# A fused group-norm and windowed-attention kernel: exponentials split by pairs of tiles, row sums moved to a bank of the row scores, the statistic put before the second maximum, the bias of V put on ScalarE

## The chip, the cores and the metric

The kernel runs on one core of a Trainium2 chip. The metric is device time in microseconds (us) of one execution, lower is better. PE is TensorE (PEld its weight loads), DVE is VectorE, ACT is ScalarE, POOL is GpSimd, SP is the engine that issues the DMAs.

## The reference

The input is x of shape (4, 128, 112, 112) in fp32. It is group-normalised (32 groups of 4 channels per image), goes through attention in shifted windows, and is added to the result. Cut to what matters:

```python
def _gn(v, G=32, eps=1e-05):           # mean and variance per image and group
    ...
xs = jnp.roll(x, (-3, -3), axis=(-2, -1))
qkv = jnp.einsum('bchw,oc->bohw', xs, w_qkv) + b_qkv[None, :, None, None]
# 16 x 16 windows of 7 x 7 = 49 tokens, 8 heads of 16 channels
scores = jnp.einsum('bxyhqd,bxyhkd->bxyhqk', q, k) * scale
attn = jax.nn.softmax(scores, axis=-1)
out = jnp.einsum('bxyhqk,bxyhkd->bxyhqd', attn, v)
...
x = x + _L0_conv_ref(_gn(x), w_qkv, b_qkv)
```

## The kernel before, in words

An image is 16 bands of 7 rows, and a band is two groups of 8 windows. So there are 4 x 32 = 128 groups, and the program is a software pipeline over them: each engine runs its own list of work, `step(g)`, in an order written out by hand, and semaphores (one counter for each kind of result, waited for with `wait_ge`) tie the lists together. PE's order sets the beat. In its step g it does, in this order:

- `project_v(g)` (L725), V of group g into the V bank,
- `sum_keys(g-2)` (L783), the sums of the exponentials over the keys, 64 fp32 matmuls (rows of the trace),
- `weigh(g-2)` (L797), exponentials times V,
- `project_q(g+1)` (L716),
- `row_scores(g, 0)` (L740), the scores of heads 0 to 3 with a query in each row, needed only for the row maximum; it waits for the masked queries (`q_masked`) and for K split in two halves (`k_split`),
- `turn_max(g-1)` (L752), `spread_inverse(g-2)` (L808),
- `column_scores(g-1)` (L765, L772), the scores again with a key in each row, the negated maximum added,
- `row_scores(g, 1)` (L740), and `project_k(g+1)` (L709).

DVE's step g: `mask_q(g)` (L564, two instructions), the statistic of the next image (`take_stats`, L487, one chunk of 448 elements; a step has one chunk, two, or none), `invert(g-2)` (L576) and `low_inverse(g-2)` (L581), `join(g-2)` (L588), `maximum(g, 0)` (L571), `low_q(g+1)` (L556), `scale_rows(g-2)` (L597), `maximum(g, 1)` (L571). ACT's step: `evac_k`, `normalise(g+2)`, `high_inverse`, `evac_even`, `evac_v`, `evac_q(g+1)`, `evac_neg(g-1)` (L368), and the two exponentials of g-1 (L373). POOL's step: `add_bias(g-3)` (L291, the bias of V added to the output), `split_max(g-1)` (L282, L285), `split_k(g)` (L273, L275: k_hi, then k_lo = k - k_hi, whose end is `k_split`), `add_image(g-3)` (L300, the residual), `split_x(g+2)` (L263, L265).

The statistics of image b+1 are gathered while image b is worked on: 28 chunks of `take_stats`, then the chain of small instructions that turns them into scale and shift. `change_image` cuts that chain over six steps, in pieces that stand at two places of the step, before `invert` (`ahead`) and before `join` (`between`). Steps 22 to 29, 54 to 61 and 86 to 93 are the eight before each new image is needed; the last image, from step 94 on, has no statistics left to take.

PSUM has 8 banks. Row scores use banks 0 and 1, Q and K bank 4, V, the turned maximum and the spread inverse bank 5. Heads 0 and 1 of the column scores are in banks 6 and 7, heads 2 and 3 in banks 2 and 3, so the first exponential (`exp(g, 0)`) takes heads 0 and 1 of all four pairs of windows, the second heads 2 and 3. The sums over the keys lie in spare columns of bank 3; `weigh` writes banks 6 and 7. SP stores each band and loads one of a later image in its place.

Of the kernel before, what the change touches and what calls it, by code (L numbers as in the profile page):

```python
# [35 lines left out]
def window_attention(nc, x, w_qkv, b_qkv, out):  # L36
# [7 lines left out]
    with ctx:  # L44
# [181 lines left out]
        def _(pool):  # L226
# [61 lines left out]
            def add_bias(g, half):  # L288
                pool.wait_ge(mixed_done, g + 2)
                pool.sem_inc(waited, 1)  # L290
                nc.gpsimd.tensor_scalar(mixed[:, half, :, :], mixed[:, half, :, :], bias[:, 2:3], None, ALU.add).then_inc(bias_added, 1)  # L291

# [24 lines left out]
            for g in range(-2, 4):  # L317
                step(g, g // 2, g & 1)
            with pool.Fori(2, GROUPS // 2 - 1) as n:
# [4 lines left out]
            for g in range(GROUPS - 2, GROUPS + 3):  # L324
                step(g, g // 2, g & 1)

        @block.scalar
        def _(act):
# [23 lines left out]

            def evac_k(g):
# [38 lines left out]
            def step(g, n, par, b=0):  # L392
# [12 lines left out]
                if live(g - 1):  # L405
                    evac_neg(g - 1)
                if live(g - 1):
# [16 lines left out]
            for g in range(GROUPS - 2, GROUPS + 2):  # L424
# [3 lines left out]
        def _(dve):  # L428
# [87 lines left out]
            def group_mean():  # L516
# [4 lines left out]
                link(nc.vector.tensor_tensor(work_b[:, :], work_a[:, :], work_a[:, :], ALU.mult))  # L521

            def group_variance():

                link(nc.vector.tensor_tensor(work_a[:, :], work_b[:, :], var_row[:, :], ALU.add))
# [3 lines left out]
            def guess_root():  # L529

# [3 lines left out]
            def refine_root(steps):  # L534

                for _ in range(steps):
                    link(nc.vector.tensor_tensor(rs_t[:, :], rs[:, :], rs[:, :], ALU.mult))
                    link(nc.vector.scalar_tensor_tensor(rs_t[:, :], rs_t[:, :], -0.5, g_var[:, :], ALU.mult, ALU.mult))
                    link(nc.vector.scalar_tensor_tensor(rs[:, :], rs_t[:, :], 1.5, rs[:, :], ALU.add, ALU.mult))

            def scatter_groups():
# [4 lines left out]
            def offer(b):  # L546

                wait(dve, xn_ready, (b - 1) * 2 * BANDS)
# [52 lines left out]
            def step(g, n, par, chunks=(), image_at=None, ahead=None, between=None):  # L601
# [11 lines left out]
                if between:  # L613
                    between()
# [6 lines left out]
                if live(g - 2):  # L621
                    scale_rows(g - 2, par)
                if live(g):
# [7 lines left out]
            def change_image(b):  # L631

                g = (b * BANDS - 4) * 2
                for ahead, between in ((None, lambda: gather_channels(b)),
                                       (turn_channels, group_mean),
                                       (group_variance, guess_root),
                                       (lambda: refine_root(1), lambda: refine_root(1)),
                                       (lambda: refine_root(NEWTON - 2), scatter_groups),
                                       (None, lambda: offer(b))):
                    step(g, g // 2, g & 1, ahead=ahead, between=between)  # L640
                    g += 1
# [9 lines left out]
            gather_channels(0)  # L651
            turn_channels()
            group_mean()
            group_variance()
            guess_root()
            refine_root(NEWTON)
            scatter_groups()
            offer(0)
# [5 lines left out]
            step(2, 1, 0)  # L664
            step(3, 1, 1)
            with dve.Fori(2, BANDS - 4) as n:
# [196 lines left out]
```

## Time and profile before

| | |
|---|---|
| median of 3 runs | 941.21 us (940.23 to 943.64) |
| the profiled execution | 941.08 us, its span 938.9 us |
| PE busy (matmul) | 865.0 us, 92% of the span |
| DVE busy | 766.3 us, 82% |
| POOL busy | 739.3 us, 79% |
| ACT busy | 665.1 us, 71% |
| DMA | 51.87 MB, mean 55 GB/s |

The span is the time from the first to the last instruction on the chip; the execution's own time is 2.2 us more. The shares of busy time are averages over the fill of the pipeline (some 72 us), 124 steps and a short drain. A busy PE here is the union of matmuls whose ends are modelled, so 92% doesn't say that PE is the only limit: two steps of the same work are best compared by their length. Line numbers are those of the kernel before.

### The profile page before, as it was taken

To read this page: it belongs to the slowest core of one execution; us is meant where nothing else is said; L and a number is where in the kernel's file an instruction comes from. 1 tells how busy PE (TensorE), PEld (TensorE's weight loads), DVE (VectorE), ACT (ScalarE), POOL (GpSimd) and SP (SyncE) were. 2 spreads that over 40 slices of the span, in tenths; PEclk is the share of its full clock that TensorE was granted. 3 is DMA by queue.
4 is the path that set the end of the run, shared out by engine and by line. 5 is a ranking of instruction groups with operands and counts; after the bars stand their busy time and mean duration, and the time that the engine had idled before them with its cause. 6 is when DMAs were issued, how large, how long until landed. Compare 5 with 4: busy or idle time off the path is not lost. (4 is left out here: it accounts for less than half of the span.)

```text
span 938.9 us, 104445 instructions
## 1 busy us (share of the span) xinstructions
PE 865.0 (92%) x46473; PEld 708.7 (75%) x46473; DVE 766.3 (82%) x1399; ACT 665.1 (71%) x1297; POOL 739.3 (79%) x1191
## 2 busy tenths in 40 slices
PE   0479999998999999999999999999899999999994
PEld 0358888887788888887788888887678888888883
DVE  8657888889889888888888888888987777777873
ACT  2347777776677777777677777777677777777772
POOL 1347888887788888888788888888788888888883
PEclk9999999999999999999999999999999999999998
DMA  9401122112112211221211000000000000000001
GB/s 380 177 5 58 46 68 68 60 42 69 48 55 68 69 43 60 68 68 34 69 54 50 35 34 34 17 34 34 17 34 35 19 32 34 34 22 29 34 34 36
DMA packets 29912, 51.87 MB, mean 55 GB/s; under 512 B 3649, under 2 KB 28865, under 8 KB 29761
## 3 DMA queue, kind: packets, MB, share of 16 engines
q1 hardware_dynamic: 29888, 51.59, 15.8%
q8 instruction: 11, 0.18, 0.1%
q14 instruction: 13, 0.10, 0.0%
HBM read 25.89 MB, written 25.69 MB: 55 GB/s over the span
## 5 line engine op out<-in xcount | busy, mean ns | idle before, releaser
L373 ACT ACTIVATE probs_t<-psum,exp_scale 128x800 f32<-128x800 f32 x256 | 223.2, 923 | 139.6 <-PE psum L772 139.6
L571 DVE TENSOR_REDUCE neg_max<-psum 100x16 f32<-100x784 f32 x256 | 249.2, 974 | 39.1 <-PE psum L740 31.1
L291 POOL TENSOR_SCALAR mixed<-mixed,bias 128x392 f32<-128x392 f32 x128 | 161.7, 1263 | 123.2 <-DVE mixed L597 123.2
L740 PEld LDWEIGHTS psum<-k_hi,q_masks 32*128 32x128 f16 x8192 | 175.3, 91 | 46.3 <-issue 42.8
L740 PE MATMUL psum<-k_hi,q_masks 32*128 32x49 f16 x8192 | 197.8, 179 | 3.0 <-DVE neg_max L571 2.3
L740 PE MATMUL psum<-k_lo,q_masks 32*128 32x49 f16 x4096 | 182.6, 179 | 0.0
L740 PEld LDWEIGHTS psum<-k_lo,q_masks 32*128 32x128 f16 x4096 | 161.0, 91 | 0.0
L300 POOL TENSOR_TENSOR stage<-mixed,image 128x343 f32 (+7 forms) x256 | 144.2, 583 | 0.4 <-POOL mixed L291 0.4
L765 PE MATMUL psum<-q_masks,k_hi 32*64 32x100 f16 x8192 | 128.7, 219 | 16.1 <-DVE summed L588 13.3
L349 ACT ACTIVATE xn<-image,shift_c,rstd_c 128x21 f32 (+6 forms) x256 | 132.4, 573 | 8.0 <-DVE shift_c L551 6.1
L797 PE MATMUL psum<-probs_t,v_rows 64*32 64x100 f32 x8192 | 131.4, 252 | 2.4 <-issue 2.4
L783 PE MATMUL psum<-probs_t,sum_rows 128*32 128x49 f32 x8192 | 117.7, 209 | 9.6 <-ACT probs_t L373 2.7
L783 PEld LDWEIGHTS psum<-probs_t,sum_rows 128*32 128x32 f32 x8192 | 103.8, 110 | 28.5 <-issue 25.2
L275 POOL TENSOR_TENSOR k_lo<-k,k_hi 128x392 f16<-128x392 f32 x128 | 116.5, 910 | 10.7
L265 POOL TENSOR_TENSOR xn_lo<-xn,xn_hi 128x392 f16<-128x392 f32 x128 | 116.2, 908 | 10.7
L564 DVE TENSOR_SCALAR q_masks<-q_halves,even_odd 128x800 f16<-128x800 f16 x256 | 120.6, 511 | 2.3 <-DMA image<-in_x_dram 2.3
L765 PEld LDWEIGHTS psum<-q_masks,k_hi 32*64 32x64 f16 x8192 | 103.5, 102 | 22.5 <-issue 17.8
L765 PE MATMUL psum<-q_masks,k_lo 32*64 32x100 f16 x4096 | 111.7, 218 | 0.0
L797 PEld LDWEIGHTS psum<-probs_t,v_rows 64*32 64x32 f32 x8192 | 102.5, 106 | 11.4 <-issue 2.8
L588 DVE SCALAR_TENSOR_TENSOR summed<-psum,v_scale,even_out 128x392 f32<-128x392 f32 x128 | 80.1, 625 | 38.1 <-ACT even_out L390 37.4
L725 PE MATMUL psum<-w_lo,xn_hi 128*128 128x128 f16 x512 | 94.9, 222 | 0.0
L725 PE MATMUL psum<-w_hi,xn_lo 128*128 128x128 f16 x512 | 94.8, 222 | 0.0
(112 smaller groups left out, 1828.2 us busy)
## 6 DMA issues: line engine op xcount, KB each, us to landing
out_dram<-stage SPq DMA_DIRECT2D x64, 224.0 KB, 2.1
out_dram<-stage SPq DMA_DIRECT2D x64, 168.0 KB, 1.9
image<-in_x_dram SPq DMA_DIRECT2D x32, 224.0 KB, 2.6
image<-in_x_dram SPq DMA_DIRECT2D x1, 6104.0 KB, 28.2
image<-in_x_dram SPq DMA_DIRECT2D x34, 168.0 KB, 2.5
image<-in_x_dram SPq DMA_DIRECT2D x6, 896.0 KB, 9.2
image<-in_x_dram SPq DMA_DIRECT2D x1, 728.0 KB, 14.3
w_nat<-in_L_conv_w_qkv_dram SPq DMA_DIRECT2D x1, 192.0 KB, 2.4
```

What stands on the lines that cost most here:

```text
L275: nc.gpsimd.tensor_tensor(k_lo[:, par, :, 0:TOK], k, k_hi[:, par, :, 0:TOK], ALU.subtract).then_inc(k_split, 1)
L291: nc.gpsimd.tensor_scalar(mixed[:, half, :, :], mixed[:, half, :, :], bias[:, 2:3], None, ALU.add).then_inc(bias_added, 1)
L300: last = nc.gpsimd.tensor_tensor(pixel_view(stage[:, bass.ds(st, BAND)], piece), token_view(mixed[:, half, :, :], piece), pixel_view(image ...
L349: last = nc.scalar.activation(token_view(xn, piece), pixel_view(image[:, bass.ds(at, BAND)], piece), ACT.Identity, bias=shift_c[:, b % 2:b ...
L373: nc.scalar.activation(probs_t[:, 2 * u:2 * u + 2, :, :].rearrange("p h a q -> p h (a q)"), psum[:, COL_BANKS[u], 0:PAIRS * ROWS2], ACT.Ex ...
L564: last = nc.vector.tensor_scalar(both[:, :, e, :], q_halves[:, :, :, :].rearrange("p l w q -> p (l w) q"), even_odd[:, e:e + 1], None, ALU ...
L571: nc.vector.tensor_reduce(neg_max[:, par, 2 * j:2 * j + 2, :], psum[0:ROWS2, ROW_BANKS, 0:GT] .rearrange("p h (w k) -> p h w k", k=TOK), A ...
L725: last = nc.tensor.matmul(psum[:, V_BANK, a * C:(a + 1) * C], xs[:, par, 2 * a:2 * a + 2, :].rearrange("p w k -> p (w k)"), wv[:, 2, :], s ...
L740: last = nc.tensor.matmul(psum[:, ROW_BANKS.start + h - 2 * j, w * TOK:(w + 1) * TOK], q_masks[rows, par, low + w * ROWS2:low + w * ROWS2 ...
L765: nc.tensor.matmul(psum[side, COL_BANKS[h // 2].start + h % 2, a * ROWS2:(a + 1) * ROWS2], k[rows, par, w, :], q_masks[rows, par, low + w ...
L783: last = nc.tensor.matmul(psum[c * PC:(c + 1) * PC, SUM_BANK, SPARE_SUM], sum_rows[:, a, e, :, :, :].rearrange("p t w s -> p (t w s)"), pr ...
L797: last = nc.tensor.matmul(psum[c * PC:(c + 1) * PC, OUT_BANKS.start + s, a * C:a * C + ROWS2], v_rows[side, par, a, c * PC:(c + 1) * PC], ...
```

## The change

Five things are edited together.

1. The banks are dealt anew: column scores in banks 4 to 7 (one for each of the four pairs of heads), V, turned maximum and inverse in bank 3, Q and K in bank 2. An exponential now covers all heads of two pairs of windows: `exp(g, 0)` pairs 0 and 1, `exp(g, 1)` pairs 2 and 3; each still reads 800 elements per partition. `sum_keys` waits for the first before its first matmul, and for the second in its middle.
2. The sums over the keys lie in the spare columns of bank 0, beside row scores. So `sum_keys(g-2)` waits for the second maximum of g-1 (`max_done[1]`), `row_scores(g, 0)` waits for `inv_done` of g-2, and `column_scores` no longer does.
3. `take_stats` and every piece of the chain (`ahead`) stand right before the second maximum; the place `between` is gone. `change_image` has eight steps in place of six, and starts two steps earlier. A step's chunks are dealt a little differently: steps 2 and 3 take one, and the four steps before each of the last two changes of image take two each (eight such steps), where before four steps in all took two.
4. `add_bias` goes from POOL to ACT, behind `evac_neg` and ahead of the exponentials.
5. `add_image` on POOL works on g-4 in place of g-3, and the pipeline's end gets a step more.

The diff, cut to its core:

```diff
-        ROW_BANKS, COL_BANKS, OUT_BANKS = slice(0, 2), (slice(6, 8), slice(2, 4)), slice(6, 8)
-        NEG_BANK, SUM_BANK, QK_BANK, V_BANK, INV_BANK = 5, 3, 4, 5, 5
+        ROW_BANKS, COL_BANKS, OUT_BANKS = slice(0, 2), slice(4, 8), slice(6, 8)
+        NEG_BANK, SUM_BANK, QK_BANK, V_BANK, INV_BANK = 3, 0, 2, 3, 3
-        SPARE_SUM = slice(PAIRS * ROWS2, PAIRS * ROWS2 + TOK)
+        SPARE_SUM = slice(GT, GT + TOK)
+        HALF = PAIRS // 2
...
             def step(g, n, par):
-                if live(g - 3):
-                    add_bias(g - 3, 1 - par)
...
-                if live(g - 3):
-                    add_image(g - 3, n - 2 + par, 1 - par)
+                if live(g - 4):
+                    add_image(g - 4, n - 2, par)
...
+            def add_bias(g, half):
+                act.wait_ge(mixed_done, g + 2)
+                nc.scalar.activation(mixed[:, half, :, :], mixed[:, half, :, :], ACT.Identity, bias=bias[:, 2:3]).then_inc(bias_added, 1)
...
-                nc.scalar.activation(probs_t[:, 2 * u:2 * u + 2, :, :].rearrange("p h a q -> p h (a q)"),
-                                     psum[:, COL_BANKS[u], 0:PAIRS * ROWS2], ACT.Exp, scale=exp_scale[:, 0:1]).then_inc(exp_done[u], 1)
+                nc.scalar.activation(probs_t[:, :, u * HALF:(u + 1) * HALF, :].rearrange("p h a q -> p h (a q)"),
+                                     psum[:, COL_BANKS, u * HALF * ROWS2:(u + 1) * HALF * ROWS2], ACT.Exp,
+                                     scale=exp_scale[:, 0:1]).then_inc(exp_done[u], 1)
...
                     evac_neg(g - 1)
+                if live(g - 3):
+                    add_bias(g - 3, 1 - par)
                 if live(g - 1):
                     exp(g - 1, 0)
...
+            def norm_steps(b):
+                return [lambda: gather_channels(b), turn_channels, group_mean, group_variance] + NEWTON * [refine_root] + [lambda: offer(b)]
...
                 if live(g):
                     mask_q(g, par)
-                if ahead:
-                    ahead()
-                for chunk in chunks:
-                    take_stats(image_at + chunk * STAT, chunk)
                 if live(g - 2):
                     invert(g - 2)
                     low_inverse(g - 2)
-                if between:
-                    between()
...
                 if live(g - 2):
                     scale_rows(g - 2, par)
+                if ahead:
+                    ahead()
+                for chunk in chunks:
+                    take_stats(image_at + chunk * STAT, chunk)
                 if live(g):
                     maximum(g, par, 1)
...
+                first = (b * BANDS - 5) * 2
+                for g, piece in enumerate(norm_steps(b), first):
+                    step(g, g // 2, g & 1, ahead=piece)
...
             def row_scores(g, par, j):
...
                     pe.wait_ge(k_split, g + 1)
+                    wait(pe, inv_done, g - 1)
...
             def column_scores(g, par):
                 wait(pe, exp_done[1], g)
-                wait(pe, inv_done, g)
...
             def sum_keys(g):
-                pe.wait_ge(exp_done[0], g + 1)
-                pe.wait_ge(exp_done[1], g + 1)
+                pe.wait_ge(max_done[1], min(g + 2, GROUPS) if isinstance(g, int) else g + 2)
                 for a in range(PAIRS):
+                    if a % HALF == 0:
+                        pe.wait_ge(exp_done[a // HALF], g + 1)
```

The program of DVE in the second step of a pass through its loop over the first image. Before, from the masks of one step to its second maximum:

```order
L564 TENSOR_SCALAR q_masks<-q_halves,even_odd 128x16x50 [waits col_mm,q_low]
L564 TENSOR_SCALAR q_masks<-q_halves,even_odd 128x16x50
L487 ISA x2
L487 BN_STATS stats<-image 128x6
L576 RECIPROCAL inv<-psum 128x49 [waits sum_mm]
L581 SCALAR_TENSOR_TENSOR inv_rows<-inv_hi,low_rows,inv 128x49 [waits inv_mm,inv_high]
L588 SCALAR_TENSOR_TENSOR summed<-psum,v_scale,even_out 128x392 [waits mixed_done,even_done]
L571 TENSOR_REDUCE neg_max<-psum 100x16 [waits neg_split,row_mm_0]
L555 REGISTER_ALU
L556 SCALAR_TENSOR_TENSOR q_halves<-psum,q_bias,q_halves 128x8x49 [waits q_high]
L597 TENSOR_TENSOR mixed<-psum,summed 128x2x4x49 [waits join_done,add_done,neg_ready,inv_mm]
L571 TENSOR_REDUCE neg_max<-psum 100x16 [waits neg_split,row_mm_1]
```

And with the change, in the same step (line numbers of the changed kernel):

```order
L561 TENSOR_SCALAR q_masks<-q_halves,even_odd 128x16x50 [waits col_mm,q_low]
L561 TENSOR_SCALAR q_masks<-q_halves,even_odd 128x16x50
L573 RECIPROCAL inv<-psum 128x49 [waits sum_mm]
L578 SCALAR_TENSOR_TENSOR inv_rows<-inv_hi,low_rows,inv 128x49 [waits inv_mm,inv_high]
L585 SCALAR_TENSOR_TENSOR summed<-psum,v_scale,even_out 128x392 [waits mixed_done,even_done]
L568 TENSOR_REDUCE neg_max<-psum 100x16 [waits neg_split,row_mm_0]
L552 REGISTER_ALU
L553 SCALAR_TENSOR_TENSOR q_halves<-psum,q_bias,q_halves 128x8x49 [waits q_high]
L594 TENSOR_TENSOR mixed<-psum,summed 128x2x4x49 [waits join_done,add_done,neg_ready,inv_mm]
L488 ISA x2
L488 BN_STATS stats<-image 128x6
L568 TENSOR_REDUCE neg_max<-psum 100x16 [waits neg_split,row_mm_1]
```

The statistic and the two instructions that set its addresses moved from behind the masks to between `scale_rows` and the second maximum.

The program of POOL at the start of a step of its loop. Before:

```order
L291 TENSOR_SCALAR mixed<-mixed,bias 128x392 [waits mixed_done]
L282 TENSOR_SCALAR neg_halves<-neg_max 100x4x8 [waits neg_mm,max_done_0,max_done_1]
L285 TENSOR_TENSOR neg_halves<-neg_max,neg_halves 100x4x8 [waits neg_high]
L269 REGISTER_ALU
L273 TENSOR_SCALAR k_hi<-k 128x8x49 [waits k_evac,col_mm]
L275 TENSOR_TENSOR k_lo<-k,k_hi 128x8x49 [waits k_high]
```

And with the change:

```order
L283 TENSOR_SCALAR neg_halves<-neg_max 100x4x8 [waits neg_mm,max_done_0,max_done_1]
L286 TENSOR_TENSOR neg_halves<-neg_max,neg_halves 100x4x8 [waits neg_high]
L270 REGISTER_ALU
L274 TENSOR_SCALAR k_hi<-k 128x8x49 [waits k_evac,col_mm]
L276 TENSOR_TENSOR k_lo<-k,k_hi 128x8x49 [waits k_high]
```

The bias is gone from the head of POOL's step; the split of the maximum, which waits for the second maximum, is the step's first instruction.

## Rows read from the trace of the kernel before

**Rows 1.** Windows of whole steps, L588 alone (one per step): us, DVE busy (x), clock, DMA

```profile
99.42:199.78 100.36, 9.39 (x15) 1.00 0.18 59
691.66:912.48 220.82, 20.67 (x33) 1.00 0.08 30
193.09:251.52 58.43, 5.00 (x8) 1.00 0.18 55
412.76:471.88 59.12, 4.99 (x8) 0.97 0.17 54
633.09:691.66 58.57, 5.00 (x8) 1.00 0.08 28
291.69:305.65 13.96, 1.23 (x2) 1.00 0.18 58
```

**Rows 2.** Timeline of one step with a statistic, PE's loads: start us, us, instruction

```profile
406.76 0.10 PEld L725 LDWEIGHTS psum<-w_lo,xn_hi 128*128 128x128 f16 x1
407.06 0.80 PEld L783 LDWEIGHTS psum<-probs_t,sum_rows 128*32 128x32 f32 x64 [0.20 <-issue]
...
409.49 0.10 PEld L740 LDWEIGHTS psum<-k_hi,q_masks 32*128 32x128 f16 x2 [0.33 <-issue]
```

**Rows 3.** Timeline of the same step, ACT

```profile
405.20 1.74 ACT L373 ACTIVATE probs_t<-psum,exp_scale 128x800 f32<-128x800 f32 x2 [0.95 <-PE psum L772]
```

**Rows 4.** Timeline of the fill, PE's loads from V to the sums

```profile
51.33 0.10 PEld L725 LDWEIGHTS psum<-w_lo,xn_hi 128*128 128x128 f16 x1
...
51.53 0.58 PEld L783 LDWEIGHTS psum<-probs_t,sum_rows 128*32 128x32 f32 x46
```

**Rows 5.** Timeline of the step of rows 2, DVE

```profile
405.04 0.56 DVE L597 TENSOR_TENSOR mixed<-psum,summed 128x392 f32<-128x392 f32 x1
405.79 0.97 DVE L571 TENSOR_REDUCE neg_max<-psum 100x16 f32<-100x784 f32 x1 [0.19 <-PE psum L740]
406.68 0.94 DVE L564 TENSOR_SCALAR q_masks<-q_halves,even_odd 128x800 f16<-128x800 f16 x2
407.55 0.61 DVE L487 BATCH_NORM_STATS2 stats<-image  x1
408.08 0.45 DVE L576 RECIPROCAL inv<-psum 128x49 f32<-128x49 f32 x1
```

**Rows 6.** Timeline of the same step, POOL

```profile
405.81 1.26 POOL L291 TENSOR_SCALAR mixed<-mixed,bias 128x392 f32<-128x392 f32 x1 [0.56 <-DVE mixed L597]
...
407.04 0.32 POOL L282 TENSOR_SCALAR neg_halves<-neg_max 100x32 bf16<-100x32 f32 x1
...
408.31 0.91 POOL L275 TENSOR_TENSOR k_lo<-k,k_hi 128x392 f16<-128x392 f32 x1
```

**Rows 7.** Timeline of the fill, a step of POOL without the bias, and the masks

```profile
60.75 0.76 DVE L564 TENSOR_SCALAR q_masks<-q_halves,even_odd 128x800 f16<-128x800 f16 x2
61.01 0.57 POOL L282 TENSOR_SCALAR neg_halves<-neg_max 100x32 bf16<-100x32 f32 x1 [1.59 <-DVE neg_max L571]
...
62.48 0.91 POOL L275 TENSOR_TENSOR k_lo<-k,k_hi 128x392 f16<-128x392 f32 x1
```

**Rows 8.** Timeline of the fill, k_lo and the row scores that wait for it

```profile
44.80 0.91 POOL L275 TENSOR_TENSOR k_lo<-k,k_hi 128x392 f16<-128x392 f32 x1
...
45.77 0.13 PEld L740 LDWEIGHTS psum<-k_hi,q_masks 32*128 32x128 f16 x2 [1.00 <-issue]
```

**Rows 9.** Timeline of the start, DVE: the chain's first instruction, and the one after its last

```profile
22.64 0.92 DVE L507 BATCH_NORM_AGGREGATE agg<-stats 128x2 f32<-128x168 f32 x1
...
28.44 0.21 DVE L478 TENSOR_SCALAR q_bias<-bias,fit 128x1 f32<-128x1 f32 x1
```

**Rows 10.** Groups by line and shape: busy us, mean ns, idle before

```profile
L390 ACT ACTIVATE even_out<-psum,v_scale 128x392 f32<-128x392 f32 x128 | 75.1, 587 | 20.8 <-PE psum L797 14.6
```

**Rows 11.** Timeline of the drain

```profile
931.53 0.57 DVE L597 TENSOR_TENSOR mixed<-psum,summed 128x392 f32<-128x392 f32 x1 [0.20 <-DVE summed L588]
932.31 1.26 POOL L291 TENSOR_SCALAR mixed<-mixed,bias 128x392 f32<-128x392 f32 x1 [5.51 <-DVE mixed L597]
933.76 1.26 POOL L300 TENSOR_TENSOR stage<-mixed,image 128x343 f32<-128x343 f32 x3 [0.18 <-POOL mixed L291]
```

More of the change, by code:

```diff
@@ L286, in split_max @@
                                         ALU.subtract).then_inc(neg_split, 1)
[L288 to L291, printed above, removed]
             def add_image(g, t, half):
@@ L311, in step @@
                     split_k(g, par)
-                if live(g - 3):
-                    add_image(g - 3, n - 2 + par, 1 - par)
+                if live(g - 4):
+                    add_image(g - 4, n - 2, par)
                 if live(g + 2):
                     split_x(g + 2, par)
-            for g in range(-2, 4):
+            for g in range(-2, 6):
                 step(g, g // 2, g & 1)
-            with pool.Fori(2, GROUPS // 2 - 1) as n:
+            with pool.Fori(3, GROUPS // 2 - 1) as n:
                 step(2 * n, n, 0)
@@ L323, in _ @@
             pool.sem_inc(x_split, 1)
-            for g in range(GROUPS - 2, GROUPS + 3):
+            for g in range(GROUPS - 2, GROUPS + 4):
                 step(g, g // 2, g & 1)
@@ L423, in _ @@
                     step(2 * n + 1, n, 1, b)
-            for g in range(GROUPS - 2, GROUPS + 2):
+            for g in range(GROUPS - 2, GROUPS + 3):
                 step(g, g // 2, g & 1)
@@ L599, in scale_rows, with step @@
                                         summed[:, :, :].rearrange("p (s a) q -> p s a q", s=2), ALU.mult).then_inc(mixed_done, 1)
-            def step(g, n, par, chunks=(), image_at=None, ahead=None, between=None):
+            def step(g, n, par, chunks=(), image_at=None, ahead=None):
                 if live(g):
                     mask_q(g, par)
-                if ahead:
-                    ahead()
-                for chunk in chunks:
-                    take_stats(image_at + chunk * STAT, chunk)
                 if live(g - 2):
@@ L650, in _ @@
                     take_stats(chunk * STAT, chunk)
[L651 to L658, printed above, removed]
+            for piece in norm_steps(0):
+                piece()
             work_out_scales()
@@ L663, in _ @@
             step(1, 0, 1, range(5, 8), BANDS * BAND)
-            step(2, 1, 0)
-            step(3, 1, 1)
-            with dve.Fori(2, BANDS - 4) as n:
-                two_steps(n, 2 * n + 4, BANDS * BAND)
+            step(2, 1, 0, (8,), BANDS * BAND)
+            step(3, 1, 1, (9,), BANDS * BAND)
+            with dve.Fori(2, BANDS - 5) as n:
+                two_steps(n, 2 * n + 6, BANDS * BAND)
             for b in (1, 2):
@@ L671, in _ @@
                 first = b * BANDS - 1
-                for n in range(3):
+                for n in range(4):
                     dve.wait_ge(loaded[b + 1], 32 * -(-(2 * n + 2) * STAT // BAND))
@@ L675, in _ @@
                 dve.wait_ge(loaded[b + 1], 32 * BANDS)
-                for g in (2 * first + 6, 2 * first + 7):
-                    chunk = 6 + 2 * (g & 1)
-                    step(g, g // 2, g & 1, (chunk, chunk + 1), at)
-                with dve.Fori(4, CHUNKS // 2 - 1) as n:
-                    two_steps(n + first, 2 * n + 2, at)
+                with dve.Fori(4, CHUNKS // 2 - 4) as n:
+                    two_steps(n + first, 2 * n, at)
+                for n in (CHUNKS // 2 - 4, CHUNKS // 2 - 3):
+                    for par in range(2):
+                        chunk = CHUNKS - 8 + 4 * (n - CHUNKS // 2 + 4) + 2 * par
+                        step(2 * (first + n) + par, first + n, par, (chunk, chunk + 1), at)
             change_image(B - 1)
@@ L764, in column_scores @@
                                 rows = slice(h * PC, (h + 1) * PC)
-                                nc.tensor.matmul(psum[side, COL_BANKS[h // 2].start + h % 2, a * ROWS2:(a + 1) * ROWS2], k[rows, par, w, :],
+                                nc.tensor.matmul(psum[side, COL_BANKS.start + h, a * ROWS2:(a + 1) * ROWS2], k[rows, par, w, :],
                                                  q_masks[rows, par, low + w * ROWS2:low + (w + 1) * ROWS2],
@@ L771, in column_scores @@
                         rows = slice(h * PC, (h + 1) * PC)
-                        last = nc.tensor.matmul(psum[:, COL_BANKS[h // 2].start + h % 2, a * ROWS2:(a + 1) * ROWS2],
+                        last = nc.tensor.matmul(psum[:, COL_BANKS.start + h, a * ROWS2:(a + 1) * ROWS2],
                                                 pick_window[rows, 2 * a:2 * a + 2, :].rearrange("p w k -> p (w k)"),
```

26 lines of the change are left out of this document (7 added, 19 removed).

## The prediction

> **What bounds the kernel now.** The page gives PE 92% and DVE 82% busy, which settles nothing, so I first cut the span into whole steps. One L588 runs per step, so its count in a window gives the length of a step [rows 1]: 15 steps with one statistic take 100.36 us, 6.69 each, and the last 33 steps, which have none, take 220.82 us, 6.69 each. A statistic on DVE costs nothing where it stands now. The eight steps before a change of image take 58.43, 59.12 and 58.57 us, together 16 us more than 24 such steps, and two steps with two statistics take 13.96, 0.58 more than two plain ones.
>
> What sets the 6.69 is read from the timeline of one step. PE goes through its phases with short gaps, and the question is which gaps are waits. From V to the sums, load to load, it takes 0.30 (406.76 to 407.06) [rows 2], and the second exponential ends at 405.20 + 1.74 = 406.94, 0.12 before [rows 3]. In the fill, with the exponentials long done, the same pair of loads is 0.20 apart [rows 4]. So 0.10 of each step is a wait for the second exponential, and the rest of the step is PE's own pace.
>
> Two other chains come close. DVE: the second maximum ends at 405.79 + 0.97 = 406.76, 0.30 before the sums [rows 5]. POOL: k_lo ends at 408.31 + 0.91 = 409.22, and the row scores start at 409.49 [rows 2, 6]. In the fill PE took up the row scores 0.06 after k_lo (45.71 to 45.77), so in a plain step k_lo has 0.27 - 0.07 = 0.20 to spare [rows 8].
>
> **The exponentials by pairs.** The first now frees the sums 0.8 earlier, the second is needed only after half of their 0.80. Each still has 800 elements, so I leave 1.74 for both. The wait goes, 0.10 per step, where nothing else is late; no step can gain more, since 0.20 is what the fill shows without a wait.
>
> **The sums in a bank of the row scores.** They now wait for the second maximum as well. It is done at 406.76, and the sums could load at 406.96: nothing in a plain step. The inversion that the next row scores wait for starts at 408.08 and lasts 0.45, a good 0.9 before them: nothing.
>
> **The bias on ACT.** An ACT pass over 392 elements takes 0.59 [rows 10]. It stands where ACT now waits 0.95 for the column scores [rows 3]; the `mixed` that it reads is a step old. The price lies between nothing and, if it took even 0.9, still nothing: I take nothing. `add_image`, a step later, is ready long before `scale_rows` needs its buffer back.
>
> **The bias off POOL.** This frees 1.26 per step, but what counts is the end of k_lo. Before, the bias runs over the first mask; the split of the maximum starts at 407.04 and k_lo ends 2.54 after the masks start (406.68) [rows 5, 6]. The fill has the same steps without a bias [rows 7]: the masks start at 60.75 and end at 61.51, L282 asks at 61.01 and needs 0.57 in place of 0.32, ending just after both masks, and k_lo ends at 63.39, 2.64 after they started. So without the bias POOL is kept out by both masks, and k_lo comes 0.10 **later**, not earlier. I take the fill's value; the bound on the other side is rival 1. In a plain step k_lo then allows the row scores 0.20 - 0.10 = 0.10 earlier than now, exactly what the exponentials give. A plain step: 6.59, and 34 of them save 34 x 0.10 = 3.4.
>
> The Trainium skill (SBUF — State Buffer, § Who interferes with whom) says that DVE in a two-port mode and GpSimd share a port pair, and that "whoever issues first gets the shared pair for the whole instruction". By that rule L282, asking while the first mask holds the pair and before the second has started, would get in between the two, and the whole would end near rival 1's time. The row at 61.01 doesn't agree on this point: it ends behind the second mask.
>
> **The statistic before the second maximum.** Every step that has one pays here. `scale_rows` starts at 405.04 and ends at 405.60; an instruction that waits for nothing starts 0.08 before its predecessor's end, so the statistic starts at 405.52. Start to start it takes 408.08 - 407.55 = 0.53, call it 0.54, and the maximum starts at 406.06 in place of 405.79: 0.27 late [rows 5]. Behind it are queued the masks, and for it wait the sums on PE and the split of the maximum on POOL. The sums: the maximum ends at 407.03, with some 0.06 on top 407.09, 0.03 later than now. k_lo: 0.27 + 0.10 late, less the 0.20 to spare, 0.17. The second is the larger, and PE loses it once (the 0.03 lies inside). A step with one statistic: 6.69 + 0.17 = 6.86. There are 58 past the fill (4 to 21, 30 to 49, 62 to 81): 58 x 0.17 = +9.9.
>
> In general a step whose piece takes p before the maximum costs p - 0.37 more than 6.69. Two statistics, p = 1.07: +0.70, 8 such steps, +5.6. The pairs of before are given back: 2 x 0.58, -1.2.
>
> **The chain at the changes of image.** Its eight pieces now stand there, in eight steps. Their bound from below is the start of the program, where DVE runs the same chain with nothing beside it: 22.64 to 28.44, 5.80 in all [rows 9]. I take it, since POOL has done its L265 by then. Eight steps: 8 x 6.69 + 5.80 - 8 x 0.37 = 56.4, three times 169.1 in place of 176.1: -7.0.
>
> **Fill and drain.** The fill's first statistics delay one maximum and free an earlier one; I take 0, with 3 either way. At the end the last `mixed` is done at 932.10 and the residual starts at 933.76, with 1.26 of bias between; with 0.59 on ACT it is 0.7 less [rows 11].
>
> **Sum.** 9.9 + 5.6 - 1.2 - 7.0 - 3.4 - 0.7 = +3.2 on the profiled execution's 941.08, so **944.3 us**. That execution is 0.1 under the median of 941.21. Within 0.5% (4.7 us) is about what a measurement can't tell from no change: 936.5 to 945.9. So the forecast is no change, on its slow side.
>
> **Rivals.**
> *1. POOL gets in between the masks.* The split of the maximum is then as fast as now, after a start of 0.14 less: k_lo about 0.2 earlier than I have it, and only the sums bind. Steps with one statistic +0.03 (1.7), with two +0.57 (4.6), changes of image 3 x (8 x 6.69 + 5.80 - 8 x 0.51) = 165.7 (-10.4), the others as above (-5.3): -9.4, **931.7**. For it: in a step with the bias L282 takes 0.32 and ends before the masks do. Against: the fill's row. Chance 0.20.
>
> *2. The statistic costs more than its own time.* In the loops two instructions that set its address precede it. If they aren't worked off under `scale_rows`, each such step pays their time before the maximum. Behind the masks they cost nothing (407.55 is 0.07 before the masks' end); the other bound is the 0.20 that DVE idles where it waits for its own last result [rows 11]. With 0.2 on 66 steps: +13, **957**. It decides early: 0.02 per step takes the time out of the 0.5%. Chance 0.12.
>
> *3. The split of the exponentials does nothing,* because the wait in the middle of the sums, or the one for the maximum at their head, holds PE as long as before. Plain steps stay at 6.69: +3.4, **947.7**. Chance 0.08.
>
> **How the numbers follow.** The forecast has 0.60, of which I give 0.40 to within 0.5%, 0.18 to slower (each 0.03 in the statistic's 0.17 is 2 us) and 0.02 to faster. Rival 1 is faster with 0.20, rival 2 slower with 0.12, rival 3 slower with 0.05 and within with 0.03. Together: faster 0.22, same 0.43, slower 0.35. The range runs from rival 1's time, rounded down, to 955, which leaves out the upper part of rival 2. The forecast's own range is 940 to 949.
>
> **What would show it.** Windows of whole steps: 6.59 in the last image, 6.86 with a statistic, 7.39 with two, 56.4 for eight steps at a change. L283 (the old L282) at about 0.57, ending behind both masks. In steps with a statistic, row scores that load 0.06 after k_lo's end, a second maximum that has no idle time before it, and no idle time of PE before the sums but for their 0.1. If L283 takes 0.3 and steps with a statistic 6.72, rival 1 holds; if the statistic starts well after `scale_rows` ends, rival 2; if the last image stays at 6.69, rival 3.

## The result, and the profile after

| | before | changed |
|---|---|---|
| median | 941.21 us (940.23 to 944.43, 5 runs) | 948.05 us (946.93 to 949.03, 5 runs) |
| the profiled execution, and its span | 941.08, 938.9 | 947.95, 946.1 |
| PE, DVE busy | 865.0, 766.3 us | 867.6, 765.6 us |
| ACT, POOL busy | 665.1, 739.3 us | 731.6, 599.0 us |

The changed kernel is slower, by little: the ratio is 1.0065, 95% interval 1.0042 to 1.0088. Over one execution the busy times tell nothing of this; POOL even lost 140 us of work. The windows of whole steps do. Here they are for the changed kernel, one L585 per step (us, DVE busy with its count, clock, DMA share, GB/s): twelve steps with one statistic, the last 33, the eight before each change of image, and four with two statistics.

```profile
101.13:183.68 82.55, 7.51 (x12) 1.00 0.19 58
701.34:920.89 219.55, 20.64 (x33) 1.00 0.08 30
197.46:253.86 56.40, 5.01 (x8) 1.00 0.18 57
420.64:477.58 56.94, 5.01 (x8) 1.00 0.17 56
644.41:701.34 56.93, 5.01 (x8) 1.00 0.08 28
391.59:420.64 29.05, 2.51 (x4) 1.00 0.17 55
```

Against [rows 1] a step with one statistic grew from 6.69 to 6.88 us, a plain step shrank from 6.69 to 6.65 (6.64 past its first), the eight steps at a change went from some 58.7 to 56.8, and a step with two statistics takes 7.26 (7.40 each, measured past the first). Each window runs from V's first load of one step to that of another. What stands before the second maximum in step g delays PE's loads of step g+1, so the first length in a window is still that of the kind of step before it.

The clock is the full 2.4 GHz in all six windows (1.00), so it has no part in the longer steps. In the kernel before, one of the three changes of image holds 3.4 us at 1.2 GHz (455.9 to 459.3; its window has 0.97 in [rows 1]) and takes 0.6 more than the other two: that much of the changed kernel's gain there isn't the change's. In the fill the clock does differ: between V's first load and that of step 4 it is 0.80 on average in the changed kernel, 0.93 in the kernel before.

The timeline of one step with a statistic (start us, us, instruction) answers to [rows 2, 5, 6]; V's first load of this step is at 329.66:

```profile
329.14 0.62 DVE L488 BATCH_NORM_STATS2 stats<-image  x1
329.67 0.96 DVE L568 TENSOR_REDUCE neg_max<-psum 100x16 f32<-100x784 f32 x1
...
330.54 0.76 DVE L561 TENSOR_SCALAR q_masks<-q_halves,even_odd 128x800 f16<-128x800 f16 x2
...
330.68 0.77 PEld L768 LDWEIGHTS psum<-probs_t,sum_rows 128*32 128x32 f32 x64 [0.20 <-DVE neg_max L568]
...
330.81 0.56 POOL L283 TENSOR_SCALAR neg_halves<-neg_max 100x32 bf16<-100x32 f32 x1 [2.06 <-DVE neg_max L568]
...
332.30 0.91 POOL L276 TENSOR_TENSOR k_lo<-k,k_hi 128x392 f16<-128x392 f32 x1
...
333.28 0.12 PEld L725 LDWEIGHTS psum<-k_hi,q_masks 32*128 32x128 f16 x2 [0.53 <-issue]
```

Read it from the top. The second maximum starts right behind the statistic, with no idle time, where before it had 0.19 of it. It ends at 330.63, and the sums on PE load 0.05 later, their wait now put down to it. The split of the maximum (L283) starts at 330.81, lasts 0.56 and ends at 331.37, 0.07 after the masks (331.30). k_lo ends at 333.21, and the row scores load 0.07 after. Their wait reads as "issue", not as POOL: only that it grew from 0.33 [rows 2] to 0.53, and always ends 0.07 after k_lo, tells that it is one.

A plain step, V's first load at 741.61, has the same pattern without the statistic. k_lo ends at 744.92, 2.66 after the masks start, and the row scores load 0.07 later:

```profile
742.26 0.76 DVE L561 TENSOR_SCALAR q_masks<-q_halves,even_odd 128x800 f16<-128x800 f16 x2
...
742.54 0.77 PEld L768 LDWEIGHTS psum<-probs_t,sum_rows 128*32 128x32 f32 x64
742.68 0.41 POOL L283 TENSOR_SCALAR neg_halves<-neg_max 100x32 bf16<-100x32 f32 x1 [1.68 <-DVE neg_max L568]
...
744.01 0.91 POOL L276 TENSOR_TENSOR k_lo<-k,k_hi 128x392 f16<-128x392 f32 x1
...
744.99 0.12 PEld L725 LDWEIGHTS psum<-k_hi,q_masks 32*128 32x128 f16 x2 [0.38 <-issue]
```

From the page's groups (busy us, mean ns of one, idle before): L283 takes 489 ns on average, where L282 took 332 in the kernel before, and the exponentials are as long as they were, 924 ns against 923.

```profile
L371 ACT ACTIVATE probs_t<-psum,exp_scale 128x800 f32<-128x800 f32 x256 | 223.5, 924 | 60.2 <-PE psum L756 60.2
L283 POOL TENSOR_SCALAR neg_halves<-neg_max 100x32 bf16<-100x32 f32 x128 | 62.6, 489 | 273.5 <-DVE neg_max L568 273.5
```

At the drain the residual starts 0.83 after the last `mixed`, in place of 1.66 [rows 11]:

```profile
939.58 0.57 DVE L594 TENSOR_TENSOR mixed<-psum,summed 128x392 f32<-128x392 f32 x1 [0.20 <-DVE summed L585]
...
940.98 1.27 POOL L296 TENSOR_TENSOR stage<-mixed,image 128x343 f32<-128x343 f32 x3 [0.26 <-ACT mixed L349]
```

### The profile page after: what moved, and what is told of

Same layout as the page of the kernel before. It is cut to its first block, busy times and chain, and to the rows that moved or that the text cites. A ratio compares the mean times of both kernels' runs of the same rounds, so it can differ in the third digit from the quotient of the medians.

```text
span 946.1 us, 104227 instructions
## 1 busy us (share of the span) xinstructions
PE 867.6 (92%) x46473; PEld 706.4 (75%) x46473; DVE 765.6 (81%) x1399; ACT 731.6 (77%) x1425; POOL 599.0 (63%) x1063
## 4 chain that ended last, share of the span: by engine, by line
PE 80%; DVE 10%; issue 5%; DMA 3%; ACT 1%; SPq 1%; POOL 0%; DVEq 0%; POOLq 0%; ACTq 0%
PE psum L725 17%; PE psum L782 13%; PE psum L768 12%; PE psum L749 10%; PE psum L700 8%; PE psum L709 7%; PE psum L693 6%; DVE neg_max L568 4%; DMA image<-in_x_dram 3%; PE psum L756 3%; PE psum L737 2%; PE psum L793 2%; DVE q_halves L553 2%; DVE mixed L594 2%; DVE stats L488 1%
## 5 line engine op out<-in xcount | busy, mean ns | idle before, releaser
L283 POOL TENSOR_SCALAR neg_halves<-neg_max 100x32 bf16<-100x32 f32 x128 | 62.6, 489 | 273.5 <-DVE neg_max L568 273.5
L725 PEld LDWEIGHTS psum<-k_hi,q_masks 32*128 32x128 f16 x8192 | 177.9, 91 | 66.6 <-issue 64.2
L578 DVE SCALAR_TENSOR_TENSOR inv_rows<-inv_hi,low_rows,inv 128x49 f16<-128x49 f16 x128 | 90.4, 706 | 49.1 <-ACT inv_hi L383 49.1
L768 PEld LDWEIGHTS psum<-probs_t,sum_rows 128*32 128x32 f32 x8192 | 99.7, 110 | 35.1 <-DVE neg_max L568 27.4
L573 DVE RECIPROCAL inv<-psum 128x49 f32<-128x49 f32 x128 | 60.2, 470 | 59.9 <-PE psum L768 59.9
L561 DVE TENSOR_SCALAR q_masks<-q_halves,even_odd 128x800 f16<-128x800 f16 x256 | 97.7, 425 | 2.6 <-DMA image<-in_x_dram 2.6
```

The costliest lines, as they stand in the source:

```text
L561: last = nc.vector.tensor_scalar(both[:, :, e, :], q_halves[:, :, :, :].rearrange("p l w q -> p (l w) q"), even_odd[:, e:e + 1], None, ALU ...
L725: last = nc.tensor.matmul(psum[:, ROW_BANKS.start + h - 2 * j, w * TOK:(w + 1) * TOK], q_masks[rows, par, low + w * ROWS2:low + w * ROWS2 ...
L768: last = nc.tensor.matmul(psum[c * PC:(c + 1) * PC, SUM_BANK, SPARE_SUM], sum_rows[:, a, e, :, :, :].rearrange("p t w s -> p (t w s)"), pr ...
```

## The experiments

The theory on trial (A) is the prediction's: the time goes through one chain, second maximum, masks, split of the maximum, k_lo, row scores; the statistic in front makes it start late, and the bias gone from POOL lets the masks' hold on POOL make it longer. The rivals are that the new banks and waits cost it, that the sums' wait for the maximum is the whole loss, and that taking work off POOL did shorten the chain. e1 to e4 ran on one chip beside 14 runs of the kernel before (median 942.25), e5 to e8 beside 12 (941.89), e9 beside 9 (940.56). The ratios below are against these. A difference from the changed kernel's 948.05 crosses sessions, whose medians of the kernel before lie within 1.7 us of each other (941.21 beside the 948.05), so it is good to a us or two; the windows of steps are firmer.

**e1, the statistic back behind the masks.** All else as in the changed kernel.

```diff
                     mask_q(g, par)
+                for chunk in chunks:
+                    take_stats(image_at + chunk * STAT, chunk)
...
                     ahead()
-                for chunk in chunks:
-                    take_stats(image_at + chunk * STAT, chunk)
```

> The changed kernel with the statistic's chunks back behind the masks; the pieces of the chain stay before the second maximum. Theory A (the changed kernel loses its time because the statistic delays the second maximum, and with it the masks, the split of the maximum on POOL, k_lo and the row scores): single-statistic steps fall from 6.88 us to the 6.64 of plain steps, two-statistic steps from 7.40 to about 6.94; 58 x 0.24 + 8 x 0.46 = 17.6 less than the changed kernel, about 930 us. Theory B (the loss comes from the new banks, the bias on ACT or the wait of the sums for the maximum): about as the changed kernel, 946 to 950.

929.21 us (927.69 to 929.44), ratio 0.9856 [0.9834, 0.9879]. Twelve steps with a statistic (first row) and the last 33:

```profile
100.54:180.20 79.66, 7.52 (x12) 1.00 0.19 60
683.74:903.24 219.50, 20.68 (x33) 1.00 0.08 30
```

Both kinds of step take 6.64. So the place of the statistic costs the changed kernel some 18.8 us, and without that one edit it beats the kernel before by 1.4%. Theory B of this run falls.

**e2, K's split ahead of the maximum's on POOL.** The statistic stays where the change put it.

```diff
             def step(g, n, par):
-                if live(g - 1):
-                    split_max(g - 1, 1 - par)
                 if live(g):
                     split_k(g, par)
+                if live(g - 1):
+                    split_max(g - 1, 1 - par)
```

> The changed kernel with POOL's split of K ahead of its split of the maximum; nothing else moves. Theory A (k_lo sets the row scores, and it is late because it is queued behind a split that waits for the late maximum and for the masks' port): k_lo no longer depends on the maximum, so only the sums' wait for the maximum is left: plain steps 6.59 to 6.60 in place of 6.64, single-statistic steps about 6.72 in place of 6.88, two statistics about 7.25, eight steps at a change about 55.2 in place of 56.8; about 932 to 933 us. L283 short, under 0.2 us. Theory B (the sums' wait for the late maximum is the loss, k_lo only follows): single-statistic steps stay at 6.85 to 6.88, time 947 to 948. Danger: the split of the maximum comes late for turn_max, then steps grow.

924.14 us (923.43 to 925.21), ratio 0.9805 [0.9783, 0.9827]. Windows as above, and the timeline of a step with a statistic (V's first load at 313.85):

```profile
98.75:178.64 79.89, 7.51 (x12) 1.00 0.19 60
681.46:898.32 216.86, 20.64 (x33) 1.00 0.08 31
```

```profile
314.74 0.75 DVE L561 TENSOR_SCALAR q_masks<-q_halves,even_odd 128x800 f16<-128x800 f16 x2
314.88 0.77 PEld L768 LDWEIGHTS psum<-probs_t,sum_rows 128*32 128x32 f32 x64 [0.20 <-DVE neg_max L568]
...
316.13 0.91 POOL L276 TENSOR_TENSOR k_lo<-k,k_hi 128x392 f16<-128x392 f32 x1
317.01 0.22 POOL L283 TENSOR_SCALAR neg_halves<-neg_max 100x32 bf16<-100x32 f32 x1
...
317.28 0.09 PEld L725 LDWEIGHTS psum<-k_hi,q_masks 32*128 32x128 f16 x2 [0.33 <-issue]
```

k_lo now ends at 317.04, 0.24 before the row scores, which are back at an idle time of 0.33. Steps with a statistic fall to 6.66, and what is left over the plain 6.56 is the sums' wait for the late maximum, 0.10. So of the 0.24 that a statistic cost, k_lo's chain carried most, and the order on POOL alone is worth 23.9 us. It came out 8 us better than expected, in good part because PE's own pace is 6.56, not 6.59, and steps with a statistic take 6.66, not 6.72. The sums' loads take 0.77 in place of 0.80 [rows 2]. They do so here too, where they wait for the maximum; in e5, where they wait for the second exponential again, they take 0.80.

**e3, both edits.**

> Both edits: statistic behind the masks, K's split ahead of the maximum's. Theory A: plain and single-statistic steps all at PE's own pace, 6.59 to 6.60, two-statistic steps under 6.95, changes of image about 55.2 per eight steps: about 922 to 924 us, faster than both kernels. Theory B: no better than the better of the two edits alone by more than 1 us.

916.39 us (915.21 to 917.44), ratio 0.9721 [0.9702, 0.9739].

```profile
99.50:178.22 78.72, 7.51 (x12) 1.00 0.19 61
673.74:890.60 216.86, 20.64 (x33) 1.00 0.08 31
```

Every step of one statistic or none takes 6.56, PE's own pace. 7.8 us better than e2 alone.

**e4, the bias back on POOL**, at the head of its step as in the kernel before, all else as in the changed kernel.

```diff
+                if live(g - 3):
+                    add_bias(g - 3, 1 - par)
                 if live(g - 1):
                     split_max(g - 1, 1 - par)
```

ACT no longer adds it.

> The changed kernel with the bias of V back on POOL, at the head of its step. Theory A (without the bias POOL's split of the maximum meets both masks and waits them out; with it the split comes in between them): plain steps fall to about 6.60 with L282's work at about 0.3 us in place of 0.49, steps with a statistic stay near 6.88, since there the split is asked for later and meets the masks all the same; about 945 to 947 us. Theory B (the bias was in POOL's way, and taking it off shortened the chain to k_lo): plain steps grow to 6.7 or more, over 950 us.

939.56 us (936.87 to 940.7), ratio 0.9961 [0.9942, 0.9979]. The timeline of a step with a statistic (V's first load at 319.81):

```profile
319.58 1.26 POOL L292 TENSOR_SCALAR mixed<-mixed,bias 128x392 f32<-128x392 f32 x1 [0.47 <-DVE mixed L595]
...
320.70 0.76 DVE L562 TENSOR_SCALAR q_masks<-q_halves,even_odd 128x800 f16<-128x800 f16 x2
...
320.96 0.23 POOL L283 TENSOR_SCALAR neg_halves<-neg_max 100x32 bf16<-100x32 f32 x1
...
322.15 0.91 POOL L276 TENSOR_TENSOR k_lo<-k,k_hi 128x392 f16<-128x392 f32 x1
...
323.24 0.09 PEld L726 LDWEIGHTS psum<-k_hi,q_masks 32*128 32x128 f16 x2 [0.33 <-issue]
```

With 1.26 us more to do per step, POOL finishes k_lo earlier: 2.36 after the masks start in place of 2.67, because L283 takes 0.23 and is done at 321.19, before the masks' end at 321.46. Moving the bias off POOL cost some 8.5 us in all. That is less than the steps alone would make it, for eight steps at a change are longer here, 57.9 to 58.6 against 56.4 to 56.9. I had the gain for plain steps only (6.56 measured, expected 6.60), and expected steps with a statistic to stay at 6.88; they fell to 6.66. In them L283 starts 0.07 before the second mask, just as in the changed kernel, and yet it gets in, in all 58 of them. Where two statistics or a piece of the chain stand in the step it doesn't, at the same distance. Here is one such step; the bias ended 0.64 before the split's start, not 0.11:

```profile
394.47 0.76 DVE L562 TENSOR_SCALAR q_masks<-q_halves,even_odd 128x800 f16<-128x800 f16 x2
394.73 0.57 POOL L283 TENSOR_SCALAR neg_halves<-neg_max 100x32 bf16<-100x32 f32 x1 [0.64 <-DVE neg_max L569]
```

e8 and e9 go after that.

**e5, both exponentials waited for ahead of the sums.**

```diff
-                for a in range(PAIRS):
-                    if a % HALF == 0:
-                        pe.wait_ge(exp_done[a // HALF], g + 1)
+                pe.wait_ge(exp_done[0], g + 1)
+                pe.wait_ge(exp_done[1], g + 1)
+                for a in range(PAIRS):
```

> The changed kernel with both exponentials waited for at the head of the sums. Theory A (the split of the exponentials is worth its 0.10 us where nothing else is late, and where a statistic makes the maximum late, nothing): the sums load at 1.02 after V's first load in plain steps in place of 0.93, row scores would start at 3.45 in place of 3.38, so plain steps 6.69 in place of 6.64 and steps with a statistic unchanged at 6.88: 34 x 0.05 = +1.7, about 950 us. Theory B (the wait in the middle of the sums costs as much as it gives): unchanged, 948 us, plain steps 6.64.

950.83 us (948.17 to 952.0), ratio 1.0096 [1.0076, 1.0116], 2.8 over the changed kernel's median; by the time alone the two can't be told apart. The last 33 steps, and the sums of one of them:

```profile
701.99:923.21 221.22, 20.67 (x33) 1.00 0.08 30
```

```profile
743.51 0.80 PEld L768 LDWEIGHTS psum<-probs_t,sum_rows 128*32 128x32 f32 x64 [0.20 <-issue]
```

The 33 plain steps make 1.7 of it. They go back to the 6.69 of before, those with a statistic stay (6.87). So the split does what it says, for 0.05 us a plain step here; the other 0.08, down to 6.56, it gives only where k_lo isn't late.

**e6, one part alone on the kernel before:** bias on ACT and residual on g-4, nothing else.

> The kernel before with nothing but the bias of V on ACT and the residual on g-4. Theory A (without the bias ahead of it POOL's split of the maximum waits both masks out, and k_lo comes about 0.10 us later, which here lies inside the 0.20 it has to spare): plain steps 6.69, L282's work about 0.5 us in place of 0.32, time 940 to 942 us, less some 0.7 to 1.2 at the drain; the bias as such is worth nothing to the steps. Theory B (freeing POOL of 1.26 us per step makes k_lo and the steps faster): steps under 6.65, under 937 us.

945.52 us (943.68 to 947.6), ratio 1.004 [1.0027, 1.0053]. The last 33 steps, the group of the split, and DVE at step 36:

```profile
699.23:920.11 220.88, 20.67 (x33) 1.00 0.08 30
```

```profile
L282 POOL TENSOR_SCALAR neg_halves<-neg_max 100x32 bf16<-100x32 f32 x128 | 62.0, 484 | 273.0 <-DVE neg_max L570 273.0
```

```profile
295.46 1.68 DVE L563 TENSOR_SCALAR q_masks<-q_halves,even_odd 128x800 f16<-128x800 f16 x2 [1.99 <-DMA image<-in_x_dram]
```

Steps stay at 6.69, with L282 at 484 ns: k_lo's delay lies inside what it had to spare, as theory A has it, and the steps gain nothing from POOL's free time. The time is 4 us more all the same, from a cost I hadn't counted: with the residual a step later, bands are stored and loaded later (the load that ends this wait is issued at 292.81, in step 36, where the kernel before issues it at 284.96, at the end of step 34), and DVE waits at steps 36 and 68 for the last band of the next image. Those two steps take 10.81 and 11.13. Behind each wait the clock is 1.2 GHz for a while, which is part of the cost:

```profile
300.70:304.00 3.30, 3.30 (x141) 2.58 (x133) 2.22 (x5) 2.31 (x4) 0.00 (x0) 0.50 0.00 0
522.50:529.20 6.70, 6.56 (x236) 5.62 (x240) 4.78 (x9) 4.78 (x9) 2.00 (x4) 0.50 0.00 0
```

(us, then busy time of PE, PE's loads, DVE, ACT and POOL, and the clock.) The changed kernel asks for the band two steps later, at steps 38 and 70, and has no such wait: its new dealing of chunks spares it this.

**e7, the chain's pieces behind the masks too**, on top of e3.

```diff
                     mask_q(g, par)
+                if ahead:
+                    ahead()
...
-                if ahead:
-                    ahead()
```

> The fastest so far (statistic behind the masks, K's split ahead of the maximum's) with the chain's pieces behind the masks too, one per step in eight steps. Theory A (behind the masks a step has some 0.8 us to spare before the inversion delays anything, before the second maximum only 0.3): eight steps at a change fall from 54.9 to about 53 us (8 x 6.56 = 52.5), 3 x 2 = 6 us less, about 911 us. Theory B (behind the masks the small instructions with two inputs meet POOL's passes and are held up by them, as the 0.79 us of L519 in the kernel before): eight steps 54 to 57 us, 915 to 922.

911.14 us (907.57 to 911.52), ratio 0.9681 [0.9667, 0.9696]. The first and third change of image:

```profile
187.08:240.45 53.37, 5.01 (x8) 1.00 0.19 60
...
610.54:664.28 53.74, 5.00 (x8) 1.00 0.08 29
```

Eight steps at a change take 53.4 to 53.7, against 54.9 in e3 and 56.8 in the changed kernel, close to eight at PE's pace (52.5). It is the fastest version here, 30.8 us under the kernel before. It uses the change's finer pieces, but at the place that `ahead` has in the kernel before. Part of its lead is in the fill, which no edit aimed at: step 4 starts at 69.0, where it starts at 72.3 in e3.

**e8, idle work on POOL in the bias's place:** three memsets of an unused tile, behind the same semaphore.

```diff
+                if live(g - 3):
+                    pool.wait_ge(mixed_done, g - 1)
+                    for part in range(3):
+                        nc.gpsimd.memset(unused[:, part, :], 0.0)
                 if live(g - 1):
                     split_max(g - 1, 1 - par)
```

> The changed kernel with three memsets of an unused tile (392 elements each, about 0.45 us each, data of no use) on POOL where the bias stood, waiting for the same semaphore; the bias itself stays on ACT. Theory A (what lets the split of the maximum in between the masks is that POOL is at work until it asks): L283 at 0.25 to 0.35 us in place of 0.49, plain steps 6.56 to 6.60, steps with a statistic 6.66, about 939 us as with the bias on POOL. Theory B (it takes an instruction that reads SBUF and itself holds up the first mask; a memset reads nothing): L283 stays at 0.5 us, steps as in the changed kernel or longer, 948 us or more.

948.5 us (947.27 to 949.24), ratio 1.0075 [1.0056, 1.0094]. A step with a statistic, and a plain one:

```profile
323.09 1.16 POOL L307 MEMSET unused<- 128x392 f32 x3 [0.32 <-DVE mixed L600]
...
324.52 0.56 POOL L284 TENSOR_SCALAR neg_halves<-neg_max 100x32 bf16<-100x32 f32 x1 [0.28 <-issue]
...
743.87 0.78 DVE L567 TENSOR_SCALAR q_masks<-q_halves,even_odd 128x800 f16<-128x800 f16 x2
744.14 0.25 POOL L284 TENSOR_SCALAR neg_halves<-neg_max 100x32 bf16<-100x32 f32 x1
```

Neither theory holds whole. Plain steps come to 6.56, with the split at 0.25; steps with a statistic stay at 6.88, with 0.56. Memsets that read nothing are enough in the one kind and not in the other. Two things differ: how long before the second mask the split starts (0.10 us in plain steps, where the memsets' end also pushes the masks a little, 0.065 in the others), and how long POOL has been idle by then (0.04 against 0.28). e9 takes the two apart.

**e9, a gap between the masks:** one more instruction on DVE, a memset of 32 elements.

```diff
                 for e in range(2):
+                    if e == 1:
+                        nc.vector.memset(unused[:, :], 0.0)
                     last = nc.vector.tensor_scalar(both...
```

> The changed kernel with a memset of 32 elements of an unused tile on DVE between the two masks. In the rows so far the split of the maximum (L283) starts 0.065 to 0.070 us before the second mask in every even step and is held until that mask's end, while in the runs where it started 0.10 or 0.17 before it got in between; in odd steps a register instruction makes it start after the second mask. Theory A (what decides is how long before the second mask POOL asks): the gap moves the second mask by about 0.06 us, so L283 gets in between in even steps alone, takes about 0.25 us there and 0.45 in odd ones; steps with a statistic alternate or average between 6.66 and 6.88, about 6.77, for some 941 to 944 us. Theory B (POOL is kept out whenever it was idle before it asks, whatever the distance): L283 lost in all steps, and all steps a little longer than 6.88 and 6.64, 949 to 954 us.

936.41 us (935.75 to 937.99), ratio 0.9957 [0.994, 0.9975]. Two steps in a row:

```profile
319.55 0.42 DVE L564 TENSOR_SCALAR q_masks<-q_halves,even_odd 128x800 f16<-128x800 f16 x1
319.93 0.09 DVE L563 MEMSET unused<- 128x32 f32 x1
319.98 0.42 POOL L284 TENSOR_SCALAR neg_halves<-neg_max 100x32 bf16<-100x32 f32 x1 [1.99 <-DVE neg_max L571]
...
326.44 0.42 DVE L564 TENSOR_SCALAR q_masks<-q_halves,even_odd 128x800 f16<-128x800 f16 x1
326.71 0.23 POOL L284 TENSOR_SCALAR neg_halves<-neg_max 100x32 bf16<-100x32 f32 x1 [2.07 <-DVE neg_max L571]
326.81 0.09 DVE L563 MEMSET unused<- 128x32 f32 x1
```

Steps alternate between 6.65 and 6.90, as theory A says: the split gets in where it starts 0.105 before the second mask (all 67 such steps, with POOL idle for 1.6 us and more before it), and not where it starts behind it. An instruction of no use, 128 times, makes the changed kernel 11.6 us faster. That is more than I expected, since the two-statistic steps and the changes of image gain as well.

## Why the prediction was right, and where it was off

The range (931 to 955) held the time, and the forecast of no change, on its slow side, came out a little too low: +0.65% where 944.3 is +0.3%, so the result lies just past the 0.5% bound, in the case that had 0.35, and inside the forecast's own 940 to 949. Here is each term of the sum beside what the two profiled spans show. Each group of steps is measured one step later at both ends (from V's first load of steps 5, 23, 31 and so on), since what a step has before its second maximum lengthens the next:

| term | predicted | measured |
|---|---|---|
| single statistics, less the pairs given back | +8.7 | +9.5 |
| steps with two statistics | +5.6 | +5.7 |
| changes of image | -7.0 | -6.4 |
| plain steps | -3.4 | -1.7 |
| fill | 0 | +1.2 |
| drain | -0.7 | -1.2 |
| sum | +3.2 | +7.1 |

The two spans differ by 7.2; the rest is rounding.

- *What bounds the kernel; the wait for the second exponential.* Right: e5 takes it back and gets the 6.69 again. The size was too small: that no step can gain more than 0.10 is not so. Plain steps in e2 to e4 take 6.56, which is 0.13 less, since the sums' loads get shorter too (0.77 against 0.80).
- *The bias off POOL makes k_lo later, by the masks.* Right, and the point that made the forecast. k_lo ends 2.66 after the masks start, forecast 2.64; e6 has the effect alone, e4 undoes it. Rival 1, that POOL gets in between, had 0.20 and fell for this kernel; for the steps its reading of what that would be worth was near: e4 shows steps with one statistic at 6.66, where it has 6.72. Its 931.7 for the whole isn't borne out, for e4 takes 939.56: the split doesn't get in at the changes of image and in steps with two statistics.
- *The statistic before the second maximum.* Right in mechanism and nearly in size: 6.88 in place of 6.86, and 7.40 in place of 7.39 with two. e1 gives the whole price of its place, 18.8 us, because it is measured against 6.64, not 6.69.
- *A plain step at 6.59.* This term was mis-sized. I let k_lo and the exponentials tie at a gain of 0.10, but k_lo comes 0.02 later than I took it, and the row scores, once they have waited for it, start their first matmul 0.03 after its load instead of at once. So a plain step gains 0.05: 1.7 of the missing 3.9 us. The same 0.03 is in the steps with a statistic.
- *The chain at the changes of image.* Nearly right: 56.6 per eight steps, forecast 56.4. The predicted -7.0 is counted from a kernel before that loses 0.6 to the clock in one of its three changes.
- *Fill at 0* was a guess with 3 either way; it cost 1.2. Over the changed kernel and the nine others, step 4 starts at 69.0 to 74.1 us with no order in it that I could find. The clock in the fill doesn't give it either: at 1.00 in e2 step 4 starts at 72.2, at 0.94 in e5 at 74.0, at 0.90 in e7 at 69.0. So this term isn't settled.
- *The bias on ACT at nothing.* Right for the exponentials, which start when the column scores are done; it takes 0.62 and stands before an idle time of 0.43 that is left.
- *Rival 2* (the statistic's address instructions) fell: the statistic starts 0.09 before `scale_rows` ends. *Rival 3* fell with e5: its 947.7 is the number nearest to the result, but by chance, for it has plain steps at 6.69, and they take 6.64.

## What to carry to other kernels

A piece of work that is hidden where it stands has a price at any other place. Read that price off the wait that ends last behind the new place; here it was a chain through three engines, not the engine that the piece moved on. Taking work off an engine doesn't help if what it does next must wait for something: look at what it will meet when it gets there sooner or idle. And before moving an instruction for a few tenths, see whether two independent instructions on a queue simply stand in the wrong order: swapping K's split and the maximum's gave 23.9 us, more than every other edit.

## What the runs showed of the hardware that I had not expected

Whether the split on POOL gets in ahead of the second of two masks on DVE goes with two things: how long before that mask's start the split's row starts, to a few hundredths of a us, and how long POOL was idle before it. Counted over the steps of each kernel, the first left out:

- Where the row starts 0.17 us or more before the second mask (the kernel before, 122 times; e4, 33; e6, 2) or 0.09 to 0.11 (e8, 33; e9, 67), it always got in between. In e6 and e9 POOL had been idle for 1.6 us and more, so idle time alone doesn't keep it out.
- At 0.06 to 0.08, with POOL idle for 0.17 us or more, it was always held until that mask's end: the changed kernel (67), e1 (67), e5 (67), e6 (67), e8 (94), e4 (36), the kernel before (5).
- At 0.07 with the bias ended only 0.11 us before, in e4's 58 steps with one statistic, it always got in.
- Where the row starts behind the start of the second mask, as in every other step of the changed kernel (60 times), it was held.

Whether it is the short idle time that lets it in in e4, or that the bias reads what the memsets of e8 don't, is open: no run has a memset that ends as shortly before, at that distance.

The Trainium skill (SBUF — State Buffer, § Who interferes with whom) gives the port pair to whoever issues first. From 0.09 us on the runs agree. At 0.07, with POOL idle before, they don't: the later instruction on DVE has it. The same page's rule that a DVE instruction with two SBUF inputs contends with a GpSimd instruction that reads SBUF agrees with the changed kernel too: L578, which reads two tiles, is 0.84 us long from 332.43, to 0.06 behind k_lo's end, and 0.53 in the plain step at 744.45, where it too ends 0.06 behind k_lo. Nothing is late by it there: the maximum that follows, at 334.12, still has 0.30 of idle time before it.
